# Adaptive layer norm, linear attention and a mixture of experts on one core: the second norm's centring moved to ScalarE, the gate turned around, the projection and statistics issued earlier

## The reference

```python
h = layernorm(x) * (1 + ca) + sa                       # x is 4 x 1024 x 128, ca, sa, ... from silu(c) @ wmod
x = x + ga * attention(h)                              # 8 heads of 16, features elu(q @ proj) + 1, blocks of 32 rows
h = layernorm(x) * (1 + cb) + sb                       # the second norm
logits = (h @ w_red) @ wg_n.T                          # 8 experts
idx, score = argmax(logits), softmax(logits)[idx]      # top 1
y = gelu(h @ w1[idx] + b1[idx]) @ w2[idx] + b2[idx]    # 128 -> 512 -> 128
out = x + gb * y * score
```

## Time and profile before

| what | value |
|---|---|
| median of the runs | 273.75 us (273.18 to 275.33) |
| the profiled execution | 273.41 us |
| its span, from first to last instruction | 271.7 us |
| TensorE busy | 246.3 us, 91% |
| VectorE busy | 223.6 us, 82% |
| ScalarE busy | 182.3 us, 67% |
| GpSimd busy | 159.2 us, 59% |
| mean granted TensorE clock | 0.992 |

### The profile page before, as it was taken

The page is one execution under the profiler, slowest core; times in us unless marked ns, Lnnn a source line. Parts: engine busy times, 40 slices in busy tenths (PEclk is TensorE's granted clock), DMA queues, the critical chain, the costliest instruction groups (busy, mean ns, idle before and its releaser), DMA issues.

```text
span 271.7 us, 11509 instructions
## 1 busy us (share of the span) xinstructions
PE 246.3 (91%) x4004; PEld 182.2 (67%) x4005; DVE 223.6 (82%) x743; ACT 182.3 (67%) x479; POOL 159.2 (59%) x199
## 2 busy tenths in 40 slices
PE   7699889999999999999999887997788999999960
PEld 3354555666766757667666565777678999999950
DVE  6778899999999999999999999687974776667640
ACT  2865657787687777868777655758866766766730
POOL 4423135174188487595771857786889974455550
PEclk9999999999999999999999999999999999999996
DMA  6910001955407218031040044222466444344300
GB/s 174 259 45 2 2 4 43 307 114 155 127 33 209 82 53 250 17 102 62 2 149 16 12 154 128 110 87 80 160 185 182 131 131 132 117 113 124 114 21 0
DMA packets 21583, 28.44 MB, mean 105 GB/s; under 512 B 3343, under 2 KB 16531, under 8 KB 21536
## 3 DMA queue, kind: packets, MB, share of 16 engines
q1 hardware_dynamic: 17920, 19.26, 25.7%
q0 software_dynamic: 3296, 8.41, 8.7%
q10 hardware_dynamic: 320, 0.13, 0.2%
HBM read 15.38 MB, written 10.64 MB: 96 GB/s over the span
## 4 chain that ended last, share of the span: by engine, by line
PE 56%; DVE 13%; issue 7%; POOL 7%; DMA 3%; SPq 1%; ACT 1%; POOLq 1%; DVEq 0%; ACTq 0%
PE ps L883 14%; PE ps L956 9%; PE ps L984 8%; PE ps L847 6%; PE ps L894 6%; DVE phi L1259 5%; PE ps L908 3%; PE ps L923 2%; POOL sorted_rows L504 2%; DMA rin<-sorted_rows 2%; PE ps L916 2%; PE ps L950 2%; PE ps L935 1%; PE ps L836 1%; POOL out L569 1%
## 5 line engine op out<-in xcount | busy, mean ns | idle before, releaser
L639 ACT ACTIVATE ebuf<-ps 128x512 f32<-128x512 f32 x128 | 69.5, 595 | 29.8 <-PE ps L883 29.5
L1259 DVE SCALAR_TENSOR_TENSOR phi<-ebuf,ps 128x512 f32<-128x512 f32 x128 | 81.1, 675 | 2.6 <-ACT ebuf L639 2.5
L883 PE MATMUL ps<-qk,proj_w 64*128 64x512 f32 x384 | 62.0, 427 | 4.9 <-DVE phi L1259 4.3
L701 ACT ACTIVATE gT<-ps,b_cols 128x128 f32<-128x128 f32 x156 | 44.6, 368 | 17.1 <-PE ps L956 13.9
L984 PE MATMUL ps<-w_sb,gT 128*128 x312 | 42.2, 278 | 4.2 <-DVE y L1553 2.8
L984 PEld LDWEIGHTS ps<-w_sb,gT 128*128 128x128 f32 x312 | 37.9, 192 | 6.1 <-issue 5.9
L883 PEld LDWEIGHTS ps<-qk,proj_w 64*128 64x128 f32 x384 | 31.2, 184 | 15.8 <-issue 4.1
L569 POOL DMA_INDIRECT out<-yo,tok x27 | 27.4, 1013 | 21.5 <-DVE yo L1569 19.0
L504 POOL DMA_INDIRECT sorted_rows<-rec,pos x32 | 32.8, 1024 | 8.5 <-issue 7.5
L894 PEld LDWEIGHTS ps<-phi 128*32 128x32 f32 x2048 | 22.5, 112 | 20.4 <-issue 13.5
L894 PE MATMUL ps<-phi 128*32 128x32 f32 x2048 | 29.6, 199 | 0.2 <-ACT a_sb L652 0.2
(11 more groups left out here) (205 smaller groups left out, 421.6 us busy)
## 6 DMA issues: line engine op xcount, KB each, us to landing
rin<-sorted_rows SPq DMA_DIRECT2D x39, 192.5 KB
vbd<-vals SPq DMA_DIRECT2D x32, 68.0 KB
w1b<-in_L_ffn_w SPq DMA_DIRECT2D x4, 512.0 KB
w_sb<-in_L_ffn_w SPq DMA_DIRECT2D x8, 256.0 KB
sorted_rows<-pad_rec SPq DMA_DIRECT2D x9, 192.5 KB, 6.0
x_all<-in_L_attn_x SPq DMA_DIRECT2D x2, 256.0 KB, 3.5
w1b<-in_L_ffn_b SPq DMA_DIRECT2D x1, 512.0 KB
sorted_rows<-rec,pos POOLq DMA_INDIRECT x32, 2.9
```

What stands on the lines that cost most here:

```text
L639: nc.scalar.activation(ebuf[:, h % 2, j, :], x_ps[h % 2][:, j, :], ACT.Exp, scale=1.0 / SHRINK, bias=math.log(SHRINK) - 1.0).then_inc(s_ex ...
L701: last = nc.scalar.activation(gT[:, b, c_, :], h_ps[b][:, j, i * P:(i + 1) * P], ACT.Gelu, bias=b1_cols[:, bass.ds(e * FC + c_, 1)])
L883: last = mm(x_ps[h % 2][:, j, :], proj_w[rows, w_part, h, :], qk_of(g, part, h // HT)[rows, :], start=w_part < part, stop=w_part == part)
L1259: last = v.scalar_tensor_tensor(out=phi[:, h % 4, j, :], in0=ebuf[:, h % 2, j, :], scalar=SHRINK, in1=x_ps[h % 2][:, j, :], op0=ALU.min, o ...
```

## The change

1. The second norm's centring goes from VectorE to ScalarE for groups 0 to 6: `center` computes h2 = x * rs + (-mean * rs) as one activation for each of the four tiles, with the scale `ln2_rs` and the bias `ln2_nb`, at h=7 on both sides of the copy `keep_v`. GpSimd makes the bias with two small operations behind the inverse, and its `norm2_scale` now multiplies by 1 + cb and adds sb, in the step of the centring and no longer at the start of the next one. The last scatter of group g-3 and `build_scale` are issued around it in another order, and GpSimd no longer waits for the pick before `take_early`. The last group keeps the old form.
2. The gate is turned around for groups 0 to 5: `w_gate`, padded with zeros from 8 to 32 columns, is stationary, and each tile's 128 transposed rows move; the four tiles write the four groups of 32 partitions of one bank. ScalarE copies the result (`keep_lgT`), TensorE transposes it (`turn_lg`, at h=4), and ScalarE copies the logits (`keep_logits`, now at h=5). Groups 6 and 7 use the old form (`gate_rows`).
3. `project_out` moves from h=5 to h=4 and to bank 6, `residual` and `norm2_stats` to h=4, `norm2_moments` to h=5, ahead of `route_max` and `route_below`; `route_first` moves to h=6; `rank` moves behind `values` at the end of h=7.

```diff
@@ GpSimd
                 rsqrt(ln2_rs[:, :], ln2_ve[:, :], s_rs2)
+                if g < NG - 1:
+                    g_.tensor_scalar(ln2_nm[:, :], ln2_mv[:, :, 0], -1.0, None, ALU.mult).then_inc(s_nm2, 1)
+                    pool.wait_ge(s_rs2, g + 1)
+                    pool.wait_ge(s_nm2, g + 1)
+                    g_.tensor_tensor(ln2_nb[:, :], ln2_nm[:, :], ln2_rs[:, :], ALU.mult).then_inc(s_nb, 1)
...
             make_tables()
+            g_.memset(w_gate[:, :], 0.0).then_inc(c_wz, 1)
...
             def norm2_scale(g, first):
-                pool.wait_ge(s_rs2, g + 1)
                 pool.wait_ge(s_nh, g + 1)
-                g_.tensor_tensor(h2[:, :, :], h2[:, :, :], ln2_rs[:, :].unsqueeze(2).broadcast_to([P, TG, D]), ALU.mult).then_inc(s_nm, 1)
+                if first:
+                    pool.wait_ge(c_one, 1)
+                g_.tensor_tensor(h2[:, :, :], h2[:, :, :], mod_bc[:, bass.ds(g // GB_, 1), 2, :].broadcast_to([P, TG, D]),
+                                 ALU.mult).then_inc(s_nm, 1)
...
-                if prev2:
-                    norm2_scale(g - 2, firstp2)
...
-                if prev3:
-                    scatter(g - 3, [3])
...
                 if is_last(g):
+                    scatter(g - 3, [3])
...
-                    pool.wait_ge(s_pick, NG - 2)
...
+                if prev:
+                    norm2_inverse(g - 1)
+                if prev3 and not is_last(g):
+                    scatter(g - 3, [3])
+                if prev:
+                    norm2_scale(g - 1, firstp)
                 if prev2:
                     build_scale(g - 2)
-                if prev:
-                    norm2_inverse(g - 1)
@@ ScalarE
+            def keep_lgT(g):
+                act.wait_ge(s_lg, g + 1)
+                nc.scalar.copy(lgT_sb, lg_ps).then_inc(s_lgt, 1)
+
+            def center(g, tiles):
+                act.wait_ge(s_nb, g + 1)
+                if not (isinstance(g, int) and g == 0):
+                    act.wait_ge(s_h2, g)
+                for t in tiles:
+                    last = nc.scalar.activation(h2[:, t, :], x2_of(g)[:, t, :], ACT.Identity, scale=ln2_rs[:, t:t + 1], bias=ln2_nb[:, t:t + 1])
+                if TG - 1 in tiles:
+                    last.then_inc(s_nh, 1)
...
                     if h == 4 and prev2:
+                        keep_lgT(g - 2)
+                    if h == 5 and prev2:
                         keep_logits(g - 2)
...
-                    if h == 5 and prev2:
+                    if h == 6 and prev2:
                         gate_exp(g - 2)
+                    if h == 7 and prev:
+                        center(g - 1, range(0, 2))
                     if h == 7 and nxt:
                         keep_v(g + 1, False)
+                    if h == 7 and prev:
+                        center(g - 1, range(2, TG))
@@ TensorE
+            def gate(g):
+                pe.wait_ge(s_h2ts, g + 1)
+                if g:
+                    pe.wait_ge(s_lgs, g)
+                for t in range(TG):
+                    last = mm(lg_ps[t * BLK:(t + 1) * BLK, :], w_gate[:, :], h2T[:, t, :], start=True, stop=True)
+                last.then_inc(s_lg, 1)
+
+            def turn_lg(g):
+                pe.wait_ge(s_lgt, g + 1)
+                nc.tensor.transpose(lg_ps, lgT_sb, ident[:, :]).then_inc(s_lt, 1)
...
             def rank(g):
                 pe.wait_ge(s_pick, g + 1)
+                pe.wait_ge(s_cr, g + 1)
...
-                    if h == 5 and prev:
-                        if prev2:
-                            pe.wait_ge(s_lgs, g - 1)
+                    if h == 4 and prev:
                         project_out(g - 1)
-                    if h == 7 and prev2:
-                        pe.wait_ge(s_x2, g)
-                        rank(g - 2)
...
+                    if h == 4 and prev2:
+                        turn_lg(g - 2)
                     if h == 7 and nxt:
                         values(g + 1)
+                    if h == 7 and prev2:
+                        rank(g - 2)
@@ VectorE
-                    if h == 4 and prev2:
-                        route_max(g - 2)
-                        route_below(g - 2)
-                        route_first(g - 2)
-                    if h == 5 and prev:
+                    if h == 4 and prev:
                         residual(g - 1)
-                    if h == 6:
-                        if prev2:
-                            score_sum(g - 2)
-                        if prev:
-                            norm2_stats(g - 1)
-                        if prev2:
-                            score_inverse(g - 2, firstp2)
+                        norm2_stats(g - 1)
+                    if h == 5:
                         if prev:
                             norm2_moments(g - 1)
+                        if prev2:
+                            route_max(g - 2)
+                            route_below(g - 2)
+                    if h == 6 and prev2:
+                        route_first(g - 2)
+                        score_sum(g - 2)
+                        score_inverse(g - 2, firstp2)
...
-                        if prev:
-                            norm2_center(g - 1, range(0, 1), firstp)
...
```

More of the change, by code:

```diff
@@ L109, in adaln_kernel @@
         wgT = sb("wgT", [GD, E])
-        w_gate = sb("w_gate", [P, E])
+        w_gate = sb("w_gate", [P, BLK])
         w1b2 = sb("w1b2", [P, E * (F + D)])
@@ L248, in adaln_kernel @@
         m_ps = ps[:, 7, :]
+        lg_ps = m_ps[:, 0:P]
+        rk_ps = m_ps[:, 0:(TG + 1) * E]
+        po_ps = ps[:, 6, :]
         row_ps = [ps[:, 7 - b % 2, :] for b in range(B)]
@@ L520, in apart, with step @@
                 g_.memset(xc[:, :, :], 0.0).then_inc(s_apart, 1)
[L522 to L524 removed]
+            def step(g, nxt=False, prev=False, prev2=False, prev3=False, firstp=False):
                 if prev3:
@@ L903, in apply_values @@
                 elif not first:
+                    if half == 0:
+                        pe.wait_ge(s_x2, g)
                     pe.wait_ge(s_on, 2 * g + half)
@@ L910, in apply_values, with project_out @@
                 last.then_inc(s_av, 1)
-            def project_out(g, bank=m_ps):
+            def project_out(g, bank=po_ps):
                 pe.wait_ge(s_ot, g + 1)
@@ L930, in turn_h2, with gate_rows @@
                 last.then_inc(s_h2t, 1)
-            def gate(g, bank=m_ps):
+            def gate(g):
[8 more added lines that the diff above has]
+                nc.tensor.transpose(lg_ps, lgT_sb, ident[:, :]).then_inc(s_lt, 1)
+            def gate_rows(g, bank):
                 pe.wait_ge(s_h2ts, g + 1)
                 for t in range(TG):
-                    last = mm(bank[:, t * E:(t + 1) * E], h2T[:, t, :], w_gate[:, :], start=True, stop=True)
+                    last = mm(bank[:, t * E:(t + 1) * E], h2T[:, t, :], w_gate[:, 0:E], start=True, stop=True)
                 last.then_inc(s_lg, 1)
@@ L940, in rank @@
                 pe.wait_ge(s_pick, g + 1)
-                mm(m_ps[:, 0:(TG + 1) * E], before[:, :], pick[:, :, :].rearrange("p t e -> p (t e)"), start=True, stop=False)
+                pe.wait_ge(s_cr, g + 1)
+                mm(rk_ps, before[:, :], pick[:, :, :].rearrange("p t e -> p (t e)"), start=True, stop=False)
                 for u in range(TG):
-                    last = mm(m_ps[:, (u + 1) * E:(TG + 1) * E], ones_b[:, :],
+                    last = mm(rk_ps[:, (u + 1) * E:(TG + 1) * E], ones_b[:, :],
                               pick[:, u:u + 1, :].broadcast_to([P, TG - u, E]), start=False, stop=(u == TG - 1))
@@ L1073, in _ @@
             slot_hidden(3)
-            gate(NG - 2)
+            gate_rows(NG - 2, m_ps)
             slot_in(4)
@@ L1082, in _ @@
             rank(NG - 2)
-            gate(NG - 1, ps[:, 6, :])
+            gate_rows(NG - 1, ps[:, 6, :])
             outer(2, 2, e_2)
@@ L1250, in setup_gate @@
                 dve.wait_ge(p_gate, 1)
-                v.tensor_copy(w_gate[:, :], m_ps[:, 0:E]).then_inc(set_gate, 1)
+                dve.wait_ge(c_wz, 1)
+                v.tensor_copy(w_gate[:, 0:E], m_ps[:, 0:E]).then_inc(set_gate, 1)
             def features(g, h):
@@ L1444, in last_head @@
                 turn_o(NG - 1, False)
-                norm2_center(NG - 2, range(TG), False)
             def step(g, prev, prev2, nxt, nxt2, firstp=False, firstp2=False):
@@ L1516, in step @@
                             last_head()
-                    if h == 7 and not is_last(g):
-                        if prev2:
-                            position_rows(g - 2)
-                        if prev:
-                            norm2_center(g - 1, range(0, 1), firstp)
-                        if prev2:
-                            position_own(g - 2)
-                        if prev:
-                            norm2_center(g - 1, range(1, 2), firstp)
-                        if prev2:
-                            position_sum(g - 2)
-                        if prev:
```

(8 more changed lines are left out.)

34 lines of the change are left out of this document (21 added, 13 removed).

## The result

The changed kernel takes **280.66 us** in the median of four runs (279.67 to 282.56) against 273.75 before (four runs as well, not three): a ratio of 1.025, 95% interval 1.018 to 1.032. I had forecast 274.1 and a range of 270.9 to 277.3. The profiled execution took 279.67, with a span of 277.4; before 273.41 and 271.7.

A forecast was written before the change was run, and what follows sets the result against it. TensorE (18.80 of 18.80 us a step) and VectorE (18.44) were taken as almost equally full. +0.5 + 0.64 + 4 x 0 - 0.75 = +0.4 took the profiled 273.41 to 273.8, median 274.1; range 270.9 to 277.3.

The forecast's parts named there:

- the centring's term: ScalarE at the step's border: four centrings take 1.19 and delay hT's projection from +3.30 to +3.54, 0.2 a step.
- T = 18.59: Middle step closed by VectorE's late pick and rank, 7.83 after the end of feats(4), before ScalarE's delay is added.
- 7.56 in the sum: GpSimd's bias ready 7.56 after the end of feats(4), that is 0.27 before the step's border.
- The slower rival: ScalarE's wait for the bias at h=7 repeats in each step, 3.4 more: 277.5 us; chance 0.17.
- 270.3 to 270.8: Faster rival: bias in time, ScalarE never holds hT, steps of 18.59, last stage keeps 2.4; chance 0.21.
- The gate: TensorE: turned gate takes 0.25 instead of 0.79, plus 0.25 for turning the logits; sign: chain piece of 0.2 to 0.3.
- TensorE's own sum: TensorE's work in a middle step: 18.80 - 0.79 + 0.25 + 0.25 = 18.51.
- The first step: Residual and statistics now come between VectorE's features 4 and 5, so feats(7) starts late: +0.5.
- the second: Second step: bias and centrings come late, hT is 1.04 late for TensorE, 19.63 against 18.99: +0.64.
- the wait that I expected to close the step: TensorE's rank, last in the step, waits for VectorE's pick, with the next step's features queued behind it.
- The last stage's -0.75: Last step: VectorE's first pair starts 0.95 earlier, 0.45 kept at ScalarE's copy, 0.29 wait gone: -0.75 in all.
- those moves hidden: GpSimd's other moves, such as h2's scale and shift at the step's start and the last scatter behind the bias, cost nothing.

The follow-up runs named there:

- number 10: Changed kernel with ScalarE centring two tiles behind the values' copy, VectorE the other two, and GpSimd's scale and shift held until the positions are done: 277.30 us, ratio 1.011.
- number 1: Changed kernel with the second norm's centring put back on VectorE, new order and turned gate kept: 277.05 us, ratio 1.009 to the kernel before.

## Why the prediction was wrong

**The step that failed is the centring's term, "I call this 0.2 a step", and under it the model of what closes a step.** The duration: four centrings with the bias, 1.65 and not 1.19. My upper bound of 1.6 nearly held it, but I took the nearer row, four scaled copies in 1.28, and took 0.1 off it. An activation with a column for the scale and a column for the bias is not the copy: 0.40 apiece in a run. That is 0.46 in the border, 0.39 at the projection. The model: I closed the step by the pick (T = 18.59) and added ScalarE's delay to it. In truth it closes through the bias. From the end of feats(4) to the end of the bias it took 113.57 - 105.83 = 7.74, and I had 7.56 in the sum, so the missing 0.61 are 0.39, 0.18 and a remainder of 0.04. Over the four middle steps this is 2.5 us, the largest part of the 5.3 by which the span missed the forecast (5.7 longer, forecast 0.4). Another 0.5 lies in the first two steps, 1.1 in the last stage's lead, and 1.2 behind the first scatter of group 6.

**The slower rival was the right mechanism with the wrong condition.** I let it decide "once the bias is ready after the next step's first feature matmul starts". The bias came 0.24 before that, and the stall repeated all the same: what counts is when the values' copy behind two centrings frees its bank for the turn of xn. By the rival's own price (3.4 for four steps) it was dearer than what came (2.5). The range was also drawn too tight for its own rivals: it ran from 270.9 to 277.3, while they were priced at 270.3 to 270.8 and 277.5.

**The gate** was right: the next scores start 0.24 after it, and the next features 0.26 after the turn; 0.25 each in the sum. In the chain its piece is 0.35, outside the 0.2 to 0.3 that I had named as a sign, but with the scores behind it it takes 0.65 where the two took 1.18: 0.53 less, against 0.54 in the sum.

```profile
104.20 0.42 PE L978 MATMUL ps<-h2T,w_gate 128*32 128x128 f32 x8
...
104.44 0.48 PE L933 MATMUL ps<-phi 128*32 128x32 f32 x32
```

```profile
107.22 0.33 PE L983 MATMUL ps<-ident,gT 128*128 128x128 f32 x1
...
107.48 0.96 PE L922 MATMUL ps<-qk,proj_w 64*128 64x512 f32 x6
```

TensorE's own sum, 18.51, was 0.1 low (18.61 busy in number 10). **The first step** (+0.62, forecast +0.5) was right, **the second** (+1.14, forecast +0.64) too short by 0.50, about the 0.46 at its border. Rank starts at 94.19, 0.1 behind the pick's end and right behind the values' product: the wait that I expected to close the step is not there. VectorE's busy time fell by 0.4 in a middle step, where I took off 1.1; what fills the rest I did not trace.

**The last stage's -0.75 became +0.4** at the first scatter of group 6 (191.79 against 187.31, with the step's start 4.09 later). VectorE's first pair came at +2.65 where I had +2.2 and the kernel before +3.14, so the lead was 0.5. Then the count of the early rows was held for 0.45 instead of 0.12, and the cast of the positions for 0.64 by GpSimd's multiplication, which this change moved there:

```profile
173.48 1.27 POOL L490 TENSOR_TENSOR h<-h,mod_bc 128x512 f32<-128x512 f32 x1 [1.76 <-ACT h L711]
...
174.14 0.64 DVE L1443 CAST pos<-posr 128x4 int32<-128x4 f32 x1
```

Also, GpSimd's chain for group 6 (scale, shift and 1.04 of build_scale, to 177.2) stood ahead of the last group's base, which ended at 178.46; I had called those moves hidden. Behind the scatters, where I had no change, another 0.7 appeared before the first late slot's rows were turned (210.50 against 205.32), in the wait for their transfer (0.89 against 0.24), and 0.5 more by the end. I have no experiment on that; the cause stays open.

## What to carry to other kernels

Before adding a stage between a norm's statistics and the next step, walk the whole loop from the new result round to itself over every engine, at the durations of the nearest operation of the same form with the same operands, and take the dearer bound where the form differs. Slack in an engine's busy time says nothing about that loop: ScalarE was idle a quarter of the step. And when a change makes an engine finish earlier, look at what the next operation will then overlap with: here two centrings fewer cost 3.5 us more, until GpSimd was made to wait.

## What the runs showed of the hardware

- Some small VectorE operations that begin under a GpSimd `TENSOR_TENSOR` over 128x512 end with it: 1.30 for 0.18 (product of two SBUF operands, in all 15 places), 1.08 for 0.17 (cast, 20 of 21), 1.25 for 0.16 (tensor_scalar over 128x8, both). Others that read only SBUF are not held: the reduction `posr` kept its 0.17 to 0.19 in 20 places, the reciprocal over 128x16 its 0.21 to 0.25 in over 150. Operations with an operand in PSUM kept their 0.17 and 0.18 in 12 places, the features their 0.65 to 0.69. GpSimd's 1.04 over 128x4 held nothing: the product at 94.32 in the kernel before took 0.18 within it, and so in twelve places over all the traces. GpSimd's memset over 128x512 (0.54), which reads nothing, held the cast to 0.55 or 0.56 in all nineteen places, but no product of two operands: more than 90 products over 128x128 that began under it kept 0.28 to 0.29.
- ScalarE's activation with scale and bias columns over 128x128: 0.49 alone, 0.88 for two, 1.65 for four.
- TensorE's granted clock differs from one execution to the next of the same kernel. Beside number 1, the kernel before took 273.1 to 273.7 with a mean clock of 0.99 and 273.6 to 276.4 at 0.974 to 0.986. The profiles show two places of a fall: one in the last step, behind 2.7 us of TensorE work in 5 (12 of 14 profiled executions with the new order and nothing filled, none of two with the old), and one at 35 to 40 us, in both orders (8 of 19), behind a stretch in which TensorE worked 3.6 to 3.7 us of 5, in the executions with the fall and without it.
